# Three seams of a graph-attention and soft-expert kernel: where the expert weights, the first slot weights and the second expert weights are loaded and rounded

## The reference

```python
x = x + gnn(layernorm(x))      # two graph attention layers: 8 heads of 128, then 1 head of 768
x = x + ffn(layernorm(x))      # soft mixture of experts:
    logits   = einsum('nd,esd->nes', x, phi)        # 4 experts x 1024 slots
    dispatch = softmax(logits, over rows)
    combine  = softmax(logits, over all slots)
    slots    = einsum('nd,nes->esd', x, dispatch)
    h        = gelu(einsum('esd,edh->esh', slots, w1) + b1)      # 384 hidden
    y        = einsum('esh,ehd->esd', h, w2) + b2
    out      = einsum('esd,nes->nd', y, combine)
```

## Time and profile before

| | |
|---|---|
| time, median of 3 | 1894.87 us (1894.81 to 1895.03) |
| profiled execution, its own time | 1895.43 us |
| its span, first to last instruction | 1893.6 us |
| TensorE busy | 1720.6 us (91%), mean granted clock 0.974 of full |
| VectorE busy | 1118.7 us (59%) |
| ScalarE busy | 859.8 us (45%) |
| GpSimd busy | 266.1 us (14%) |
| transfers | 108.41 MB, 57 GB/s over the span |

### The profile page before, as it was taken

One profiled execution on the slowest core, in us unless ns is written; L12 is line 12 of the kernel. 1 busy time (PEld: TensorE's weight loads), 2 busy tenths in 40 slices (PEclk: granted clock), 3 DMA queues, 4 the chain that ended last, 5 costly groups with the idle time before them and its releaser, 6 DMA issues. The chain is left out here.

```text
span 1893.6 us, 30144 instructions
## 1 busy us (share of the span) xinstructions
PE 1720.6 (91%) x9905; PEld 999.8 (53%) x9905; DVE 1118.7 (59%) x1768; ACT 859.8 (45%) x1358; POOL 266.1 (14%) x116
## 2 busy tenths in 40 slices
PE   3988999689999989889997899999999968998899
PEld 2444444366655646545553555556565645665555
DVE  7998777589999936332231355555555555655311
ACT  2257888688888827311111333333333325555200
POOL 1000000178878614000000000000000000000000
PEclk9999999989999989999999999999999988999899
DMA  6000000002222240110000112221111124330421
GB/s 239 23 1 0 29 0 1 0 25 33 35 46 33 21 147 1 55 62 34 34 26 24 62 67 73 71 72 68 65 65 65 65 73 158 111 109 29 151 67 48
DMA packets 49619, 108.41 MB, mean 57 GB/s; under 512 B 16526, under 2 KB 18664, under 8 KB 49420
## 3 DMA queue, kind: packets, MB, share of 16 engines
q1 hardware_dynamic: 49484, 107.38, 18.5%
q10 hardware_dynamic: 64, 0.08, 0.0%
HBM read 79.02 MB, written 28.43 MB: 57 GB/s over the span
## 5 line engine op out<-in xcount | busy, mean ns | idle before, releaser
L829 POOL TENSOR_TENSOR base<-s_row,ln_c 128x1250 f32<-128x1250 f32 x80 | 227.5, 2846 | 56.1 <-DVE top L884 55.2
L728 PE MATMUL fs<-one_src,one_dst 128*128 x1062 | 210.1, 342 | 25.5 <-ACT one_dst L656 14.6
L93 PE MATMUL di_l<-x2t_hi,ph_hi 128*128 128x512 f16 (+1 forms) x576 | 196.3, 341 | 12.4 <-DVE ph_lo L1471 11.0
L94 PE MATMUL di_l<-x2t_lo,ph_hi 128*128 128x512 f16 (+1 forms) x576 | 196.2, 341 | 0.0
L95 PE MATMUL di_l<-x2t_hi,ph_lo 128*128 128x512 f16 (+1 forms) x576 | 196.1, 340 | 0.0
L588 DVE TENSOR_SCALAR one_src<-iota,src 128x1280 f16 x354 | 171.1, 549 | 38.9 <-PE fs L728 32.1
L953 PE MATMUL at_o<-pt,h 128*128 128x384 f32 (+1 forms) x480 | 186.0, 525 | 0.0
L728 PEld LDWEIGHTS fs<-one_src,one_dst 128*128 x1062 | 101.5, 96 | 133.4 <-issue 108.7
L940 PE MATMUL at_t<-ident,q 128*128 128x128 f32 x800 | 108.5, 285 | 29.0 <-ACT q L863 28.2
L93 PE MATMUL co_c<-ps_hi,hid_hi 128*128 128x305 f16 (+1 forms) x384 | 115.3, 300 | 21.2 <-DVE ps_lo L1698 20.6
L940 PEld LDWEIGHTS at_t<-ident,q 128*128 128x128 f32 x800 | 93.1, 146 | 73.8 <-ACT q L863 64.8
(11 more groups left out here) (242 smaller groups left out, 3278.4 us busy)
## 6 DMA issues: line engine op xcount, KB each, us to landing
logits_t<-lg SPq DMA_DIRECT2D x32, 625.0 KB, 3.6
logits_in<-logits_t SPq DMA_DIRECT2D x32, 625.0 KB, 4.1
phf<-in_phi SPq DMA_DIRECT2D x32, 384.0 KB, 3.9
s_row<-a_rows SPq DMA_DIRECT2D x9, 640.0 KB, 5.9
ew1f<-in_fw SPq DMA_DIRECT2D x6, 768.0 KB, 5.1
wf<-in_fw SPq DMA_DIRECT2D x12, 384.0 KB, 6.9
xs<-in_x SPq DMA_DIRECT2D x10, 384.0 KB, 4.0
res<-in_x SPq DMA_DIRECT2D x10, 384.0 KB, 3.0
```

Source lines behind the costliest of these rows:

```text
L93: eng.matmul(out, lh, rh, start=first, stop=False, skip_group_check=True)
L94: eng.matmul(out, lh, rl, start=False, stop=False, skip_group_check=True)
L728: mm = eng.matmul(counts(j)[:, a:a + n], one_dst[:, ds(slot(pair, m) + i, 1), :], one_src[:, ds(slot(pair, m) + i, 1), a:a + n], start=Fal ...
L829: eng.tensor_tensor(base[:, k % 2, 0:N], s_row[:, head % 2, 0:N], ln_c[:, j, 0:N], ALU.add)\
```

## The change

Three places where one kind of work ends and the next begins are rearranged.

1. In second_layer, only the first three expert weight tiles are split ahead of norm(0). Tiles 3 and 4 are split between norm(0) and norm(1), tile 5 between norm(1) and norm(2).
2. In second_layer's tail, `inputs(9)` writes to other PSUM banks (the last three of the five) and no longer waits for `xw_out` of tile 8 to be emptied. The first tile of `phi` is loaded after the last expert weight tile, ahead of the stores of the rows in SyncE's queue, and split before high_x2(9) on ScalarE and after low_x2(9) on VectorE. `phf` and `ph` get an address which second_layer no longer uses by then. In dispatch the load and split of the first tile fall away, and those of the second stand in the first loop step.
3. In combine, SyncE loads the twelve second expert weight tiles, two behind the logits loads of each of the groups 1 to 6, to free addresses. SyncE's loop is written out. In expert_outputs the weights are split first, the small pieces after them, and TensorE waits for the small pieces only behind the weight products of its first row tile. All weight loads now share one semaphore.

```diff
@@ second_layer, SyncE @@
                 eng.dma_start(ew1f[:, k % 2, :], fw1[:, k, :]).then_inc(in_ew1[k % 2], 16)
+            eng.wait_ge(q_ready, NT)
+            eng.dma_start(phf[:, 0, :, :], phi[0, :, :, :]).then_inc(in_phi[0], 16)
@@ second_layer, ScalarE (VectorE the same with low_ew1) @@
-            for k in range(KD):
+            def high_ew1(k):
...
+            for k in range(KD // 2):
+                high_ew1(k)
             for j in range(NT):
+                if j == 1:
+                    high_ew1(3)
+                    high_ew1(4)
+                if j == 2:
+                    high_ew1(5)
                 if j >= 1:
                     high_x2(j - 1)
...
+            eng.wait_ge(in_phi[0], 16)
+            eng.activation(ph[0][:, 0, :, :], phf[:, 0, :, :], ACT.Copy, scale=S_WEIGHT).then_inc(ph_hi, 1)
             high_x2(NT - 1)
@@ second_layer, VectorE @@
             low_x2(NT - 1)
+            eng.wait_ge(ph_hi, 1)
+            eng.scalar_tensor_tensor(ph[1][:, 0, :, :]..., phf[:, 0, :, :]..., S_WEIGHT, ...).then_inc(ph_lo, 1)
             low_xw(NT - 2)
@@ second_layer, TensorE @@
-        xw_out = turned
+        def xw_out(j):
+            return turned if j < NT - 1 else five[:, 2:5, :].rearrange("p b n -> p (b n)")
...
             def inputs(j):
                 eng.wait_ge(x2_lo, j + 1)
-                if j >= 1:
+                if 1 <= j < NT - 1:
                     eng.wait_ge(xw_lo, j)
@@ dispatch, SyncE, ScalarE, VectorE @@
+        def more_phi(s):
+            return valid(s + 1) and not (isinstance(s, int) and s < 0)
-                if valid(s + 1):
+                if more_phi(s):
@@ combine, SyncE @@
-            groups(eng, load, lambda G, v: None)
+            load(0, 0, 0)
+            for G in range(GROUPS):
+                for i in range(1, STEPS):
+                    load(G, G % 2, i)
+                if G + 1 < GROUPS:
+                    load(G + 1, (G + 1) % 2, 0)
+                if 1 <= G < GROUPS - 1:
+                    for k in range(2 * G - 2, 2 * G):
+                        eng.dma_start(wf[k][:, :], fw2[:, k, :]).then_inc(in_w, 16)
@@ expert_outputs @@
-            for k in range(K):
-                eng.dma_start(wf[:, k, :], fw2[:, k, :]).then_inc(in_w[k], 16)
...
+            eng.wait_ge(in_w, 16 * K)
+            for k in range(K):
+                eng.activation(wt[0][:, k, :], wf[k][:, :], ACT.Copy, scale=S_WEIGHT).then_inc(wt_hi, 1)
             eng.activation(st[0][:, :], slot_sums[:, :], ACT.Copy).then_inc(small_hi, 1)
             eng.wait_ge(in_b, 16)
             eng.activation(bt[0][:, :], bf[:, :], ACT.Copy, scale=S_WEIGHT).then_inc(small_hi, 1)
-            for k in range(K):
-                eng.wait_ge(in_w[k], 16)
-                eng.activation(wt[0][:, k, :], wf[:, k, :], ACT.Copy, scale=S_WEIGHT).then_inc(wt_hi, 1)
...
@@ expert_outputs, TensorE @@
             eng.wait_ge(ones_ready, 1)
-            eng.wait_ge(small_lo, 2)
...
+                if isinstance(t, int) and t == 0:
+                    eng.wait_ge(small_lo, 2)
                 for c in range(2):
                     split_product(eng, yp[:, u, c * BANK:c * BANK + G],
                                   [q[:, ds(t * P, P)] for q in st],
```

More of the change, by code:

```diff
@@ L193, in build @@
     z = [mem(f"z_{q}", [P, NT, D], F16) for q in ("hi", "lo")]
-    second_layer(nc, mem, sem, const, ln_c, pt, h1t, z, v2, x2t, xw, w2t, fw1, gb2, x, scratch["a2"],
-                 scratch["x1"])
+    in_phi = [sem(f"in_phi{i}") for i in range(2)]
+    ph_hi, ph_lo = sem("ph_hi"), sem("ph_lo")
+    phf, ph, after_phi = second_layer(nc, mem, sem, const, ln_c, pt, h1t, z, v2, x2t, xw, w2t, fw1, gb2, x,
+                                      scratch["a2"], scratch["x1"], phi, in_phi, ph_hi, ph_lo)
     mem.at = temps
     running_max = mem("running_max", [P, NP], F32)
+    end_running = mem.at
     hid = [mem(f"hid_{q}", [P, ST, HID], F16) for q in ("hi", "lo")]
@@ L956, in _, with second_layer @@
                         mm.then_inc(out_done, 1)
-def second_layer(nc, mem, sem, const, ln_c, pt, h1t, z, v2, x2t, xw, w2t, fw1, bias, x_in, a_rows, x_out):
+def second_layer(nc, mem, sem, const, ln_c, pt, h1t, z, v2, x2t, xw, w2t, fw1, bias, x_in, a_rows, x_out, phi,
+                 in_phi, ph_hi, ph_lo):
     RING = 4
@@ L1203, in _, with low_ew1 @@
             add_bias(1)
-            for k in range(KD):
+            def low_ew1(k):
                 eng.wait_ge(ew1_hi, k + 1)
@@ L1241, in norm @@
                                   ALU.subtract, ALU.mult).then_inc(normed_ready, 1)
+            for k in range(KD // 2):
+                low_ew1(k)
             for j in range(NT):
+                if j == 1:
+                    low_ew1(3)
+                    low_ew1(4)
+                if j == 2:
+                    low_ew1(5)
                 if j >= 1:
@@ L1332, in _, with dispatch @@
             inputs(NT - 1)
-def dispatch(nc, mem, sem, const, x2t, xw, phi, fb1, running_max, hid, logits, slots_top, max_rows):
-    phf = mem("phf", [P, 2, KD, P], F32)
-    ph = [mem(f"ph_{q}", [P, 2, KD, P], F16) for q in ("hi", "lo")]
+    return phf, ph, after_phi
+def dispatch(nc, mem, sem, const, x2t, xw, phi, fb1, running_max, hid, logits, slots_top, max_rows,
+             phf, ph, after_phi, in_phi, ph_hi, ph_lo):
     lg = mem("lg", [P, 2, N], F32)
@@ L1574, in _, with combine @@
             run(eng, step)
-def combine(nc, mem, sem, top, hid, comb, slot_sums, lt, logits):
+def combine(nc, mem, sem, top, hid, comb, slot_sums, lt, logits, wf, late_at, fw2, in_w):
     STEPS = STE // 2
@@ L1587, in combine @@
     sum_row = mem("sum_row", [P, 2, HALF], F32)
+    assert mem.at <= late_at
+    mem.at = late_at
+    wf = wf + [mem(f"wf2_{k}", [P, D], F32) for k in range(len(wf), EXPERTS * KH)]
     sums_dram = nc.dram_tensor("slot_sums", [EXPERTS * STRIPS, N], F32).ap()
@@ L1756, in _, with expert_outputs @@
                 group(2 * pair + 1, 1)
-def expert_outputs(nc, mem, sem, comb, slot_sums, wf, wt, fw2, fb2, x1, out):
+    return wf
+def expert_outputs(nc, mem, sem, comb, slot_sums, wf, wt, in_w, fb2, x1, out):
     K = EXPERTS * KH
```

49 lines of the change are left out of this document (31 added, 18 removed).

## The result

The changed kernel takes 1863.84 us, the median of 4 runs (1863.2 to 1868.39), against 1894.84 for the kernel before on the same chip (4 runs, 1893.22 to 1895.03). The ratio is 0.9843 with a 95% interval of 0.983 to 0.9855, a gain of 31.0 us. The forecast was 1864.1, in the range 1860.3 to 1869.5. The profiled execution took 1863.45 us at a mean granted clock of 0.982.

The account below looks back on a forecast made before the run. The prediction took TensorE, busy 91% of the span, as the bound, with time lost in waits and slow clock at three seams. Gains of 12.29 + 12.56 + 5.88 = 30.73 us gave 1864.1 us, range 1860.3 to 1869.5.

Parts of the forecast that it names:

- Seam 1, the wait: Norms of second_layer: with three weight tiles ahead of the row update, attend(1) starts 10.86 us earlier, about 2.0 idle stay.
- The covers: Norms of second_layer: postponed weight tiles 3 to 5 and the row loads finish before needed, tile 4 with 3.6 us spare.
- Seam 1, the clock: attend(1) in second_layer: 1.43 us lost to the lower clock level counted as gained.
- the clock falls at the waits that stay: Rival: one to three falls, 1.7 us each, at norm(0), attend(2) and inputs(8) waits; 1865.8 to 1869.2 us; chance 0.2.
- a lower clock after the 2.8 us waits: Sign that would show the prediction wrong: reduced clock behind the remaining 2.8 us waits, at attend(2) and inputs(8).
- Seam 2, idle time: Tail of second_layer: 3.54 us wait before inputs(9) goes, plus 1.70 clock inside it; dispatch starts 7.15 us earlier.
- the one that called this wait harmless from one profile: Wait before inputs(8) in the tail: its 2.77 us cost nothing in the trace, so no clock fall was priced there.
- Seam 2, the clock at dispatch: Start of dispatch: clock cost falls from 1.87 to 1.70 us behind four idle microseconds, gain 0.17, bounds 0 and 1.87.
- Seam 3: Second expert weights in expert_outputs: TensorE starts 5.06 us earlier, plus 0.82 us of clock, 5.88 us together.
- Combine's logits: Weight loads added in combine cost nothing: logits have 20 us from issue to use, against 7.7 us longest landing.
- The likeliest case: All three seams give their gains, for 1864.1 us, with clock bounds 1860.3 to 1865.9; chance 0.67.
- the clock rival: Clock falls one to three times behind the second_layer waits that stay, 1.7 us each: 1865.8 to 1869.2 us; chance 0.2.

Follow-up runs that it names:

- e1_norms: Kernel before with only the first expert weights' split spread between the norms; 0.9936 of the kernel before, 1095.57 us from attend(0) to the end.
- e11_after: The changed kernel run again unaltered on another chip; 1880.52 us, 0.9838 of the kernel before.
- e6_phi: Kernel before with only the first phi tile loaded and split early, in the tail; 0.9963 of the kernel before.
- e2_tail: Kernel before with only the tail changed, own banks for inputs(9) and early phi; 0.9901 of the kernel before.
- e8_update: Changed kernel with VectorE's row update moved out of norm(j), ahead of low_x2(j-1); 1878.35 us, 0.9833 of the kernel before.
- e4_order: Kernel before with second expert weights split first, small pieces last, loads still issued on entering expert_outputs; 0.9995 of the kernel before.
- e10_both: Changed kernel with the row update ahead of low_x2(j-1) and the other PSUM banks given to inputs(8); 1873.8 us, 0.9813 of the kernel before.
- e9_banks8: Changed kernel with the other PSUM banks given to inputs(8), not inputs(9); 1875.16 us, 0.9816 of the kernel before.
- e12_two: Changed kernel with earlier row update, other banks for inputs(8), and only two weight tiles ahead of norm(0); 1870.93 us, 0.9805 of the kernel before.

## Why the prediction was right, and where it was not

**Seam 1, the wait.** Right: 10.95 us gained against 10.86, with 1.90 us of idle time left where 2.0 was forecast. The covers held. VectorE in the kernel after, from the last tile ahead of the norms to tile 5:

```profile
795.47 1.76 DVE L1237 SCALAR_TENSOR_TENSOR ew_lo<-ew1f,ew_hi 128x1536 f16<-128x1536 f32 x1 [4.07 <-ACT ew_hi L1146]
797.14 1.01 DVE L1256 SCALAR_TENSOR_TENSOR res<-sl_b,factor,res 128x768 f32<-128x768 f32 x1
...
801.19 3.55 DVE L1237 SCALAR_TENSOR_TENSOR ew_lo<-ew1f,ew_hi 128x1536 f16<-128x1536 f32 x2 [0.30 <-ACT ew_hi L1146]
...
809.67 0.96 DVE L1243 TENSOR_TENSOR x2t_lo<-sl_b,x2t_hi 128x768 f16<-128x768 f32 x1 [4.93 <-ACT x2t_hi L1151]
...
815.06 1.75 DVE L1237 SCALAR_TENSOR_TENSOR ew_lo<-ew1f,ew_hi 128x1536 f16<-128x1536 f32 x1
```

Tiles 3 and 4 were split back to back by 804.7, and VectorE then stood idle for 4.93 us before `low_x2(0)`; 3.6 was forecast. Tile 5 followed at 815.06, and no row of the trace has VectorE waiting for a residual row.

**Seam 1, the clock.** The 1.43 us of attend(1) were gained (1.42). What the forecast had not was that the clock fell one wait later, at attend(2): 1.67 us lost. This is the rival "the clock falls at the waits that stay", and it came true at two of the three waits it names. It was also a sign of being wrong that the prediction named, a lower clock after the 2.8 us waits. Nor was it chance of one execution: in all three profiles in which attend(1) kept its clock and the wait of 2.82 us stayed (the change, e1_norms, e11_after), attend(2) lost 1.68 us. In seven of the eight others with that wait, the kernel before among them, attend(1) lost 1.4 to 2.2 us and attend(2) none; in e6_phi both lost. One of each kind, attend(1) and attend(2) with the transposes behind each, e1_norms first and then e2_tail; 9.76 us from start to transposes is the full clock:

```profile
806.55 0.39 PE L93 MATMUL sl_b<-z_hi,pt 128*128 128x512 f16 x1 [1.80 <-DVE res L1252]
...
816.31 0.82 PE L1341 MATMUL sl_b<-ident,normed 128*128 128x128 f32 x6
...
819.95 0.39 PE L93 MATMUL sl_b<-z_hi,pt 128*128 128x512 f16 x1 [2.82 <-DVE res L1252]
...
831.39 0.82 PE L1341 MATMUL sl_b<-ident,normed 128*128 128x128 f32 x6
```

```profile
823.91 0.61 PE L93 MATMUL sl_b<-z_hi,pt 128*128 128x512 f16 x1 [12.81 <-DVE res L1251]
...
835.35 0.82 PE L1340 MATMUL sl_b<-ident,normed 128*128 128x128 f32 x6
...
838.99 0.39 PE L93 MATMUL sl_b<-z_hi,pt 128*128 128x512 f16 x1 [2.82 <-DVE res L1251]
...
848.75 0.82 PE L1340 MATMUL sl_b<-ident,normed 128*128 128x128 f32 x6
```

So the clock term of this seam was mis-sized: by these three profiles it is about -0.25 us and not +1.43, until e8_update's edit removes the second wait. Why the fall moves was not isolated.

**Seam 2, idle time.** inputs(9) starts with no wait and the kernel's 1.70 us of clock inside it are back: its stretch has clock 1.00. Dispatch starts on the fill of `p` after 3.79 us, where the forecast had 4.0. That much is right. The 11.16 us instead of 12.39 come from inputs(8), which took 13.00 us to the first product of inputs(9) (993.36 to 1006.36) instead of 11.70, behind the same 2.77 us wait. The step that failed here is the one that called this wait harmless from one profile; the ten others show a fall behind it.

**Seam 2, the clock at dispatch.** This term was mis-sized: 0.17 forecast, 1.83 measured. The step that failed is the one that read a cost for four microseconds of idle time from a wait of 3.42. In the profiled execution the clock did not fall at all there. Five of the eight profiles with this wait show that it often does, at 1.7 to 2.9 us, so the term has no single size.

**Seam 3.** Right in both parts: 4.97 us against 5.06 for the start, 0.91 against 0.82 for the clock. The clock term was the mean of three unlike waits, so its closeness is partly luck: the other profiles with this wait of 7.3 us have 0.8 to 1.6 us less than the kernel before in this row tile. VectorE and ScalarE of the kernel after:

```profile
1723.95 8.91 ACT L1877 ACTIVATE wt_hi<-wf 128x768 f16<-128x768 f32 x12 [4.48 <-PEq L1670]
...
1724.83 10.52 DVE L1886 SCALAR_TENSOR_TENSOR wt_lo<-wf,wt_hi 128x768 f16<-128x768 f32 x12 [5.57 <-ACT wt_hi L1877]
...
1736.66 0.94 DVE L1891 SCALAR_TENSOR_TENSOR bt_lo<-bf,bt_hi 16x768 f16<-16x768 f32 x1
```

TensorE starts 1.98 us after the first ScalarE instruction (2.0 forecast). The last small part is done at 1737.6, and TensorE comes to the small pieces at 1739.70: covered by 2.1 us, where 1.4 was forecast, and e4_order shows what the uncovered case costs.

**Combine's logits.** Landing went from 4.1 to 4.6 us at the median, and the longest stayed at 7.6. Priced at nothing, and nothing it is.

**The sum.** The forecast of 30.73 us and the 30.08 measured are closer than their parts. The three clock errors, -1.67, about -1.3 and +1.66, cancel all but 1.3 us of each other, and the rest of dispatch gives 0.49 back. The medians differ by 31.0, the profiled spans by 32.0 of which 1.93 lie ahead of the change; how much of that the other executions share is not known. The sound part of the prediction is the idle time, each term of it right to 0.3 us; that the total fell 0.3 us from the median is luck in the clock. The likeliest case was named at 0.67 and the clock rival at 0.2; the trace shows a mixture of both, with the time of the first.

## What to carry to other kernels

At a seam between stages, look at what the late engine does just before the instruction the other waits for: work that is needed later may stand in the way, and moving half of it by one step is enough if the queue of its loads is followed too. A change of order in front of a load can be worth nothing without the load: e4_order has the one without the other and gains nothing. Price idle time from the trace, but price the clock behind it as a range for each wait that stays: a single profile can hold the rare case, as the kernel before did at inputs(8). And measure pieces by stretches of the profile, since several microseconds of difference came from blocks that no edit touched.

## What the runs showed of the hardware

How long TensorE had waited did not by itself decide whether the granted clock fell to its lower level of 1.2 GHz. Behind 1.80 to 1.92 us before attend(1) it stayed up in the change, in e1_norms, e11_after, e8_update and e10_both, and fell in e9_banks8 behind 1.96. Behind the 2.77 us wait before inputs(8) it stayed up in the kernel before and fell in all ten other profiles that have it. Behind 2.82 us before attend(2) it fell in four of eleven, in three of them where attend(1) had kept its clock, and stayed up in the seven others, where attend(1) had lost some. Behind 3.79 us at the start of dispatch it cost nothing in the change, e2_tail and e12_two, 1.7 us in e6_phi and e10_both, 2.5 in e11_after, 2.7 in e8_update and 2.9 in e9_banks8. What decides between these was not isolated; the same kernel (the change and e11_after) went both ways at this last wait, so it is not the program's order alone. One fall costs 1.3 to 2.9 us here, about as much as such a wait itself, and a few of them could make the spread between executions: of the change's four, three took 1863.2 to 1864.23 us at a mean clock of 0.981 to 0.982, and one 1868.39 at 0.977. The Trainium skill (TensorE: Matmul & The Clock Gate, Part 1: The HAM clock gate) says that in one and the same kernel the number of slow products at its start differs from run to run; these runs show the like for the falls inside a kernel.

The other surprise lies in blocks that no edit touched. The first product of attend(0) is at 788.31 us in the kernel before and at 786.38 in the change, and between 794.83 and 804.47 in the twelve experiments. Most of it shows as one wait in the first layer. GpSimd, ahead of its sums `base`, stood idle for VectorE's `top` for 53.1 us in the change and for 64.4 in e11_after, the same kernel on another chip. The groups of instructions in the first 680 us show it (last column: idle time ahead of them, and its releasers), first in the change:

```profile
L838 POOL TENSOR_TENSOR base<-s_row,ln_c 128x1250 f32<-128x1250 f32 x80 | 227.5, 2845 | 54.5 <-DVE top L893 53.1 <-DMA s_row<-a_rows 0.6
```

And e11_after:

```profile
L838 POOL TENSOR_TENSOR base<-s_row,ln_c 128x1250 f32<-128x1250 f32 x80 | 227.6, 2846 | 65.5 <-DVE top L893 64.4
```

Why VectorE is later there was not looked into. From attend(0) to the end the change and e11_after differ by 3.9 us, 2.5 of it the fall at the first logits.
